# Attention and feed-forward block on one core: first keys fetched by row tile, values copied by ScalarE and their bias added at attention's output

## The reference

```python
tp = _swiglu(time_emb @ w_t1 + b_t1) @ w_t2 + b_t2
shift1, scale1, shift2, scale2 = jnp.split(tp, 4, axis=-1)
h = _rmsnorm(x, g1) * (1.0 + scale1[:, None, :]) + shift1[:, None, :]
x = x + _mha(h, w_qkv, b_qkv, w_ao, b_ao, n_head)
h = _rmsnorm(x, g2) * (1.0 + scale2[:, None, :]) + shift2[:, None, :]
x = x + _ffn(h, w_fc, b_fc, w_fo, b_fo)
```

## Time and profile before

| | us |
|---|---|
| median of 3 runs | 3267.48 |
| lowest and highest | 3260.66, 3269.02 |
| the profiled execution | 3263.67 |
| its span, first to last instruction | 3261.9 |
| TensorE busy in the span | 3083.3 (95%) |
| VectorE busy | 1876.9 (58%) |
| ScalarE busy | 1518.4 (47%) |
| GpSimd busy | 1717.1 (53%) |
| mean granted TensorE clock | 0.972 of full |

### The profile page before, as it was taken

The page is one execution under the profiler, slowest core; times in us unless marked ns, Lnnn a source line. Parts: engine busy times, 40 slices in busy tenths (PEclk is TensorE's granted clock), DMA queues, the critical chain, the costliest instruction groups (busy, mean ns, idle before and its releaser), DMA issues.

```text
span 3261.9 us, 39659 instructions
## 1 busy us (share of the span) xinstructions
PE 3083.3 (95%) x15073; PEld 2088.2 (64%) x15073; DVE 1876.9 (58%) x2979; ACT 1518.4 (47%) x2791; POOL 1717.1 (53%) x737
## 2 busy tenths in 40 slices
PE   6996889999999999999999988799999999999999
PEld 6775665555555555555555544478888888888887
DVE  3665768787877888787787867443333333222222
ACT  2222237676767777676676756532322222111111
POOL 3453458888888888887888977632222210000000
PEclk9898999999999999999999989899999999999999
DMA  4455459899898998989889897732223201122110
GB/s 174 152 171 149 138 139 197 177 203 189 183 199 177 201 195 186 201 178 186 188 185 207 177 200 163 161 94 79 84 77 95 86 1 58 52 78 78 52 52 26
DMA packets 170638, 456.14 MB, mean 140 GB/s; under 512 B 23873, under 2 KB 57745, under 8 KB 138641
## 3 DMA queue, kind: packets, MB, share of 16 engines
q0 software_dynamic: 32256, 234.90, 36.2%
q1 hardware_dynamic: 136368, 213.21, 22.3%
q10 hardware_dynamic: 1824, 5.51, 0.4%
HBM read 140.03 MB, written 78.64 MB: 67 GB/s over the span
## 4 chain that ended last, share of the span: by engine, by line
PE 44%; POOL 22%; DMA 20%; issue 9%; DVE 3%; ACT 1%; SPq 1%; POOLq 0%; DVEq 0%; ACTq 0%
DMA b_pt<-b_pt 17%; POOL b_acc L802 16%; PE e_g L1413 10%; PE e_a L1413 10%; PE e_y L1423 10%; POOL b_acc L790 3%; PE b_s L887 3%; PE b_o L935 2%; PE e_p L1358 2%; PE b_m L871 2%; POOL a_q_lo L313 2%; PE a_qk L470 1%; POOL a_yq L306 1%; DMA b_qs<-scratch_qk_lo 1%; PE a_c L438 1%
## 5 line engine op out<-in xcount | busy, mean ns | idle before, releaser
L819 DVE TENSOR_REDUCE b_mpart<-b_m 128x1 f32<-128x512 f32 x1960 | 1200.2, 680 | 327.0 <-PE b_m L871 327.0
L770 ACT ACTIVATE b_pt<-b_s 128x512 f32<-128x512 f32 x2048 | 1088.9, 601 | 425.3 <-PE b_s L887 381.0
L802 POOL TENSOR_TENSOR b_acc<-b_acc,b_pt 128x2048 f32<-128x2048 f32 x224 | 1042.8, 4655 | 205.4 <-DMA b_pt<-b_pt 204.6
L887 PE MATMUL b_s<-b_qs,b_ks 98*128 98x512 f32 x2048 | 857.4, 421 | 57.2 <-ACT b_pt L770 33.3
L871 PE MATMUL b_m<-b_ks,b_qs 96*128 96x512 f32 x1960 | 760.2, 408 | 0.0
L887 PEld LDWEIGHTS b_s<-b_qs,b_ks 98*128 98x128 f32 x2048 | 392.0, 192 | 385.3 <-issue 191.0
L935 PE MATMUL b_o<-b_pt,b_vg 128*32 128x512 f32 x4096 | 504.0, 610 | 0.0
L871 PEld LDWEIGHTS b_m<-b_ks,b_qs 96*128 96x128 f32 x1960 | 375.2, 191 | 126.6 <-DVE b_mpart L819 54.2
L1297 DVE SCALAR_TENSOR_TENSOR e_u_lo_f<-e_a,keep_chan,e_u_lo_f 128x512 f32<-128x512 f32 x128 | 96.0, 750 | 539.0 <-PE e_a L1413 539.0
L1413 PE MATMUL e_g<-e_h_hi,e_w 128*128 128x512 f32 x1024 | 340.7, 394 | 27.9 <-DVE e_w_lo L1289 19.8
L1413 PE MATMUL e_a<-e_h_hi,e_w 128*128 128x512 f32 x1024 | 337.8, 391 | 0.0
(11 more groups left out here) (131 smaller groups left out, 3054.7 us busy)
## 6 DMA issues: line engine op xcount, KB each, us to landing
b_pt<-b_pt POOLq DMA_DIRECT2D x224, 1024.0 KB, 8.2
scratch_qk_hi<-a_q_hi SPq DMA_DIRECT2D x64, 256.0 KB
scratch_qk_lo<-a_q_lo SPq DMA_DIRECT2D x64, 256.0 KB
b_qs<-scratch_qk_hi SPq DMA_DIRECT2D x64, 256.0 KB, 6.8
b_ks<-scratch_qk_hi SPq DMA_DIRECT2D x32, 512.0 KB, 6.6
scratch_v<-a_vsb SPq DMA_DIRECT2D x32, 256.0 KB, 2.6
b_qs<-scratch_qk_lo SPq DMA_DIRECT2D x32, 256.0 KB, 9.7
b_ks<-scratch_qk_lo SPq DMA_DIRECT2D x16, 512.0 KB, 8.6
```

The costliest lines, as they stand in the source:

```text
L770: act.activation(pt[:, kt % RING, h, :], ps_s[:, score_place(i) % LEAD, :], ACT.Exp, scale=SCALE).then_inc(p_ready, 1)
L802: pool.tensor_tensor(acc[u % 2][:], acc[u % 2][:], pt[:, (2 * n + 3) % RING, :, :], ALU.add).then_inc(pool_added, 1)
L819: dve.tensor_reduce(mpart[n % 2][:, i // 4, i % 4:i % 4 + 1], ps_m[:, at, :], AX.X, ALU.max).then_inc(max_done, 1)
L887: pe.matmul(ps_s[:, place % LEAD, :], ks[n // NJ % 2][0:QR, h, kt * P:(kt + 1) * P], qs[n % 4][0:QR, h, :], start=True, stop=True).then_in ...
```

## The change

Four edits. The keys of the first four units (one group of heads, all 2048 rows) are fetched in four pieces, one behind each of tiles 0 to 3, three DMAs each; the queries of the two first units go with tiles 0 and 1. For these fetches SyncE waits for the tile's keys to be stored (keys_stored), not for its values. The values are copied out of PSUM by ScalarE, interleaved with its rounding of h, and without the bias. The bias of the values is fetched as four rows of per-channel constants (C_BV) and added to attention's normalised output, by ScalarE where that is rounded and by VectorE where the remainder is taken; that remainder moves from GpSimd to VectorE (round_off), in the first tile in VectorE's old place, and for the others behind value at step f = 1. The counts that TensorE waits for change with the number of key DMAs.

```diff
-C_ALL = C_BFC + 2 * F // P
+C_BV = C_BFC + 2 * F // P
+C_ALL = C_BV + KT
...
+    def keys_stored(eng, blk):
+
+        for i in range(2):
+            eng.wait_ge(hi_stored[i], 32 * (NP // 2 * (blk + 1) + 1))
+            eng.wait_ge(lo_stored[i], 32 * (NP // 2 * (blk + 1) + 1))
+
     def stored(eng, blk):
 
-        for i in range(2):
-            eng.wait_ge(hi_stored[i], 32 * (NP // 2 * (blk + 1) + 1))
-            eng.wait_ge(lo_stored[i], 32 * (NP // 2 * (blk + 1) + 1))
+        keys_stored(eng, blk)
+        for i in range(2):
             eng.wait_ge(v_stored[i], 16 * (SUB // 2 * (blk + 1) + 1))
...
+        sp.dma_start(rows[C_BV:C_BV + KT, :], io["b_v"].rearrange("(m p) -> m p", p=P)).then_inc(rows_in, 16)
...
-            if blk == FIRST_AT - 1:
-                stored(sp, blk)
+            if blk < FIRST_AT:
+                keys_stored(sp, blk)
                 sp.wait_ge(t2_done, 2)
-                first["loads"](sp)
+                first["loads"](sp, blk)
...
-        act.dma_start(bv[:], io["b_v"].rearrange("(o n) -> o n", o=1).broadcast_to([P, D])).then_inc(bc_in, 16)
...
+        def read_values(blk, i):
+            act.wait_ge(v_ps, SUB * blk + i + 1 + 4)
+            act.wait_ge(v_stored[i % 2], 16 * (SUB // 2 * blk + i // 2 + 1))
+            act.activation(vsb[:, i % 2, :], bank(("v", blk, i)), ACT.Copy).then_inc(v_ready, 1)
...
-            if blk + 1 < TILES:
-                for c in range(KT):
-                    round_h(blk + 1, c)
+            for i in range(SUB):
+                if blk + 1 < TILES and i % 2 == 0:
+                    for c in (i, i + 1):
+                        round_h(blk + 1, c)
+                read_values(blk, i)
...
-                dve.wait_ge(v_ps, SUB * blk + i + 1 + 4)
-                dve.wait_ge(v_stored[i % 2], 16 * (SUB // 2 * blk + i // 2 + 1))
-                dve.tensor_tensor(vsb[:, i % 2, :], bank(("v", blk, i)), bv[:], ALU.add).then_inc(v_ready, 1)
...
-    def first_loads(sp):
-        for u in range(2):
-            load_queries(sp, u)
-        for half in range(2):
-            for r in range(3):
-                load_keys(sp, 0, 0, r, half)
+    def first_loads(sp, tile):
+
+        if tile < 2:
+            load_queries(sp, tile)
+        at = slice(tile * TB, (tile + 1) * TB)
+        for r, src in enumerate((qk_hi, qk_lo, qk_hi)):
+            sp.dma_start(f32(ks[0][r * HD:(r + 1) * HD, :, at]), src[1, 0][:, :, at]).then_inc(k_in[0], 16)
...
-        pe.wait_ge(k_in[u // NJ % 2], 96 * (u // NJ // 2 + 1))
+        pe.wait_ge(k_in[u // NJ % 2], 96 * (u // NJ // 2 + 1 + (u // NJ % 2 == 0)))
...
-            for k in range(KT):
-                pool.wait_ge(ohi_ready, KT * c + k + 1)
-                pool.tensor_tensor(oa[:, k, :], oa_f[:, k, :], f32(ob[:, k, :]), ALU.subtract).then_inc(olo_ready, 1)
...
-        act.activation(ob[:, k, :], oa_f[:, k, :], ACT.Copy).then_inc(ohi_ready, 1)
+        act.activation(ob[:, k, :], oa_f[:, k, :], ACT.Identity, bias=chan[:, C_BV + k:C_BV + k + 1]).then_inc(ohi_ready, 1)
...
+    def round_off(dve, c):
+        for k in range(KT):
+            dve.wait_ge(ohi_ready, KT * c + k + 1)
+            dve.scalar_tensor_tensor(oa[:, k, :], oa_f[:, k, :], chan[:, C_BV + k:C_BV + k + 1], f32(ob[:, k, :]),
+                                     ALU.add, ALU.subtract).then_inc(olo_ready, 1)
...
                 value(nq, nf, 0 if more or f < NF - 1 else 1)
+                if more and f == 1:
+                    round_off(dve, c)
```

More of the change, by code:

```diff
@@ L114, in stage_a @@
     ps_qk, ps_c, ps_tv = m.banks(("qk", 3), ("c", 2), ("tv", 3))
-    names = ("rows_in", "bc_in", "ident_done", "rowsT", "chan_ready", "t1_done", "link", "hb_ready", "gate_ready", "zt_ready",
+    names = ("rows_in", "ident_done", "rowsT", "chan_ready", "t1_done", "link", "hb_ready", "gate_ready", "zt_ready",
              "t2_done", "whi_done", "wlo_ready", "x_in", "ss_done", "ms_ready", "sqrt_done", "own", "rstd_ready", "xn_done",
              "xT_done", "hf_ready", "hhi_done", "h_ready", "qk_ps", "prod_ready", "yq_ready", "hi_ready", "lo_ready", "v_ps", "v_ready")
-    (rows_in, bc_in, ident_done, rowsT, chan_ready, t1_done, link, hb_ready, gate_ready, zt_ready,
+    (rows_in, ident_done, rowsT, chan_ready, t1_done, link, hb_ready, gate_ready, zt_ready,
      t2_done, whi_done, wlo_ready, x_in, ss_done, ms_ready, sqrt_done, own, rstd_ready, xn_done,
@@ L163, in finished @@
         eng.wait_ge(v_ready, SUB * TILES + 2)
-    def stored(eng, blk):
+    def keys_stored(eng, blk):
         for i in range(2):
@@ L169, in stored @@
             eng.wait_ge(lo_stored[i], 32 * (NP // 2 * (blk + 1) + 1))
+    def stored(eng, blk):
+        keys_stored(eng, blk)
+        for i in range(2):
             eng.wait_ge(v_stored[i], 16 * (SUB // 2 * (blk + 1) + 1))
@@ L266, in round_q @@
                 act.activation(q_hi[:, p % 2, half, :], yq[:, p % 2, half, :], ACT.Copy).then_inc(hi_ready, 1)
+        def read_values(blk, i):
+            act.wait_ge(v_ps, SUB * blk + i + 1 + 4)
+            act.wait_ge(v_stored[i % 2], 16 * (SUB // 2 * blk + i // 2 + 1))
+            act.activation(vsb[:, i % 2, :], bank(("v", blk, i)), ACT.Copy).then_inc(v_ready, 1)
+        act.sem_inc(v_ready, 2)
         squares(0)
@@ L330, in vector @@
         dve.sem_inc(prod_ready, 8)
-        dve.sem_inc(v_ready, 2)
         count = [0]
@@ L411, in vector @@
                 conditions(1)
-                dve.wait_ge(bc_in, 16)
             for i in range(SUB):
@@ L442, in tensor @@
         pe.wait_ge(ident_done, 3)
-        pe.wait_ge(rows_in, 7 * 16)
+        pe.wait_ge(rows_in, 8 * 16)
         pe.transpose(ps_c[:, 0, 0:C_ALL], rows[:], ident[0:C_ALL, 0:C_ALL]).then_inc(rowsT, 1)
@@ L1261, in head_vector @@
             dve.tensor_tensor(wo_lo[:], wo_f[:], f32(wo_hi[:]), ALU.subtract).then_inc(wo_ready, 1)
-            for k in range(KT):
-                dve.wait_ge(ohi_ready, k + 1)
-                dve.tensor_tensor(oa[:, k, :], oa_f[:, k, :], f32(ob[:, k, :]), ALU.subtract).then_inc(olo_ready, 1)
+            round_off(dve, 0)
             dve.wait_ge(bias_in, 32)
@@ L1472, in build @@
         top = 205 * KB
-        keep = {"chan": m.sb("chan", [P, C_ALL], top), "cond_ab": m.sb("cond_ab", [P, NB, 4, KT], top + 320),
-                "ident": m.sb("ident", [P, P], top + 448), "ones": m.sb("ones", [P, P], top + 960)}
+        keep = {"chan": m.sb("chan", [P, C_ALL], top), "cond_ab": m.sb("cond_ab", [P, NB, 4, KT], top + 352),
+                "ident": m.sb("ident", [P, P], top + 512), "ones": m.sb("ones", [P, P], top + 1024)}
         b = stage_b(nc, whole, io, keep, scratch)
```

1 line of the change is left out of this document (removed).

## The result

The change takes 3216.96 us, median of four runs (3209.19 to 3228.56), beside 3268.25 for the kernel before on the same chip (3260.66 to 3269.37, four runs): a ratio of 0.9851, 95% interval 0.9817 to 0.9885. The forecast was 3225 us, with 3213 to 3243 as its range. The profiled execution took 3215.83, 47.84 less than that of before.

The account below looks back on a forecast made before the run. TensorE bounds attention and feed-forward; the loss lies in its stops in the projections' second half, 234 to 450 us. 19.5 + 16.9 + 3.4 - 0.5 = 39.3 us off 3263.67 gives 3224, set at 3225; range 3213 to 3232, with rivals 1 and 2 3243.

Parts of the forecast that it names:

- Keys (forecast 19.5 us): Projections: keys fetched by row tile cut TensorE's 20.24 us stop; 19.5 us won, bounds 14.5 and 22.5.
- a residual of 3.0: TensorE's wait for keys: a stop of 1.5 us, plus 1.5 of clock, was expected to remain.
- the long stop: TensorE's 20.24 us wait for the first unit's keys, with 2.3 us of lost clock charged behind it.
- Values on ScalarE (16.9): Projections, tiles 4 to 6: stops of 5.60, 5.18 and 0.97 us go with their clock, 16.9 us won.
- the end of the projections (3.4): Tile 7, before attention: first score about 449.5 instead of 452.89, 3.4 us won, bounds 0 and 3.4.
- the 2.13 kind: TensorE's three projection stops like the 2.13 us one at 280.93, from the root's refinement; claimed to stay.
- Bias and remainder (-0.5): Attention's output: VectorE's four remainders just fit before the matmul; 0.5 us lost for all seven tiles.
- Attention as long as before: Sign of being right: attention still takes 1638 us or so, so the earlier start passes to the end.
- 1 (last keys late, a stop of 5.7): Third key load lands at 252.5; keys win 14.5, total 34 us, time 3230; chance 0.15.
- 2 (VectorE the next bound): Projections: late reductions lengthen stops like 280.93, half of part 2 is lost, time 3233; chance 0.11.
- 3 (early loads push out the stores of q): Projections: q's rounding waits for its slot, 25 us given back, time 3250; chance 0.06.
- 4 (slower, VectorE and GpSimd meet): Output tiles: four remainders each wait 1.37 us for a GpSimd addition; 52 us, time 3277; chance 0.04.

Follow-up runs that it names:

- the keys alone: The kernel before with only the fetches changed (keys by row tile, queries with tiles 0 and 1, narrower wait): 3238.22 us, ratio 0.9929.
- the values alone: The change with queries and keys fetched in one burst behind tile 3, as before: 3242.03 us, ratio 0.9938.
- the forced tile: Tile of the change with GpSimd's additions of x held until VectorE's first remainder is taken, in tiles 1 to 7: 3228.11 us, ratio 0.9891.

## Why the prediction was right, step by step

**Keys (forecast 19.5 us).** Right in mechanism, small by some 2 us. By themselves the keys brought the first score forward by 21.3 us. I had left a residual of 3.0: a stop of 1.5 and as much of clock. The stop was 0.51, 1.00 and 1.42 us in three profiles of the change, and the clock cost behind it was nothing: granted 1.00 in the row at 248.40. The term that was mis-sized is the clock behind a short stop. The clock behind the long stop, charged at 2.3, was about right: from the end of that stop to the end of the projections' matmuls is 176.1 us before and 174.1 with the keys alone, 2.1 less. The narrower wait, which I priced at up to 2.4 us, is worth under 1: undone, the stop is 0.62 us and the time the same. The gain comes from the bytes moved to earlier tiles.

**Values on ScalarE (16.9) and the end of the projections (3.4).** Together 20.3 were forecast, and the values by themselves brought 22.7. The first term is right to the first decimal, closer than its parts deserve: from the end of the keys' stop to the end of the projections' matmuls is 176.1 us before (267.07 to 443.20) and 159.2 with the values alone (264.94 to 424.18), 16.9 less. One small piece in it had no ground: I had given 0.4 us of clock to the stop of 0.97 us, and the clock behind it was 1.00 (403.9 to 409.9 us). The end is as worked out: before, TensorE went idle at 443.20 (449.32 less 6.12) and scored at 452.89, 9.69 us later; with the values alone it took 6.02 from idle to score, 3.7 won, and in the change 6.24 (406.02 to 412.26), 3.45 won. The other 2.1 us of the 22.7 came before, and by luck: the keys' stop was 0.9 us shorter (19.33), and TensorE reached it at 245.6 instead of 246.8, where the unchanged kernel's second profile reached it at 248.0. The three stops of the 2.13 kind stayed, as said.

**Bias and remainder (-0.5).** It fits as forecast: 2.8 us expected for four remainders, 2.73 measured, 0.45 us ahead of the matmul, waits of 0.8 us in one profile and none in two, and no difference in the medians when the remainder is left on GpSimd. What was said of the removed L1103, that it clears the place for u's remainder, is shown by 777 and 705 ns. No run shows the 0.5 us itself, which is less than the medians can tell.

**Attention as long as before.** Here lies the gap between 3225 and 3217: of the 8.5 us by which the profiled execution beat its forecast of 3224, 6.6 are attention's, 1.2 the feed-forward part's and 0.8 the projections'. The change did not make attention shorter. In the eleven profiles that keep the burst of loads it took 1634.7 to 1656.1 us, with the kernel before at 1646.2 and 1634.7 and the three of the change at 1639.6, 1642.7 and 1648.2; the wait for the last queries alone ran from 7.8 to 14.6 us. The forecast held because attention does not give the early start back, and its centre missed by chance in that stage. Against the runs of before beside it, the change won 51.3, 44.1 and 39.4 us in its three measurements, and the forecast of 42.5 lies among them. Its ratio, 3225 to 3267.48, is 0.987, between the 0.9851 and the 0.9881 measured for the change at different times.

**The rivals.** 1 (last keys late, a stop of 5.7) did not come: at most 1.42 us in the change's profiles, 2.44 in one of a later version. 2 (VectorE the next bound) did not: the stops of 2.1 us neither grew nor became more. 3 (early loads push out the stores of q) did not: no wait of the projections for q's rounding, with the DMA share at 0.48 as before. 4 (slower, VectorE and GpSimd meet) came by itself in one tile, for 0.48 us, and is real when forced, but its price was too high in two terms: a meeting cost 1.0 us, not 1.37, and behind the stops of 1.5 us no clock was lost, where I had added 2.3 for each tile. The third term, four meetings a tile, was not made to happen: only two met, and the part got 12 us longer where 52 were forecast for four. At the measured price four meetings would be 4 us late, less 0.45, some 25 us for seven tiles; that is an estimate, and no run shows it.

The rule behind that rival, from the Trainium skill, SBUF — State Buffer, section Who interferes with whom, says that the later of the two is blocked for the whole of the other's instruction. The traces agree on the block: in the first tile one remainder of the same form took 5.05 us where GpSimd's fold of 5.32 us ran, instead of 0.75 (the four took 7.04), and ended 0.55 us behind the fold's end. In the forced tile the third remainder began 0.5 us behind the start of an addition and ended 0.55 us behind its end (2163.56, 2164.11):

```profile
1974.12 7.04 DVE L1261 SCALAR_TENSOR_TENSOR e_oa<-e_oa_f,keep_chan,e_ob 128x512 fp32r<-128x512 f32 x4
...
1973.30 5.32 POOL L811 TENSOR_TENSOR b_acc<-b_acc,b_pt 128x2048 f32<-128x2048 f32 x1
```

So in a sequence of short operations each waits for what is left of the other engine's, and not for a whole one: 1.0 us of an addition that takes 1.28 by itself.

## What to carry to other kernels

Where a stage ends in a transfer, spread the transfer behind the tiles that produce its parts before tightening the wait ahead of it: the bytes moved were worth 21 us, the tighter wait under 1. An evacuation that may wait for a store belongs in the queue of an engine with slack, not in the one that frees TensorE's banks. Where a profile shows one TensorE wait on a load behind a burst, look in the issuing queue for what can go one unit later. Before a few us are credited to a change, profile the same kernel more than once: attention took 1646.2 and 1634.7 us in two profiles of the same kernel here. And before an experiment is said to have forced a case, count in its trace how often the case came.
